# A two-layer gated attention network on one core: the hand-over from the first stage to the expert stage, with fifteen loads moved from GpSimd's DMA queue to SyncE's, one load moved later and one wait added on GpSimd

## The chip, the cores and the metric

One core of a Trainium2 chip runs the whole program. The metric is the device time of one execution in microseconds (us); smaller is better. The core has TensorE (PE in the rows; PEld is its weight load), VectorE (DVE), ScalarE (ACT), GpSimd (POOL) and SyncE (SP, which here only issues DMAs). Sixteen DMA engines carry the transfers of all queues. Queue q1 holds what SP issues, q10 what ACT issues, q0 what POOL issues.

## The reference, cut to what matters

The input is x, 4 x 512 rows of 256 float32 numbers, and a context of the same shape. Four residual blocks follow one another:

```python
x = x + tanh(g_xattn[0]) * L0_xattn(layernorm(x), ctx, ...)      # attention over the 16 places of a head, per row
x = x + tanh(g_ffn[0])   * L0_ffn(layernorm(x), ...)             # shared expert + one of 8 experts per row (argmax)
x = x + tanh(g_xattn[1]) * L1_xattn(ctx, ctx, layernorm(x), ...) # attention over the 512 rows of a batch entry
x = x + tanh(g_ffn[1])   * L1_ffn(layernorm(x), ...)             # butterfly weights, 256 -> 1024 -> 256
```

An expert is `gelu(x @ w1) * (x @ w2) @ w3` with 256 x 1024, 256 x 1024 and 1024 x 256 weights (3 MB). Each row goes through the shared expert and through the expert with the largest of 8 logits. The butterfly block multiplies small 2 x 2 weights stage by stage; the kernel folds these stages into dense matrices once, from tables of coefficients.

## The kernel before, in words

Rows are cut into 16 tiles of 128 (`T = 16`). The order of the work is written out by hand for each engine; engines meet at semaphores alone.

**First stage (about 0 to 331 us of the profiled span).** `sweep_a` runs a software pipeline over the tiles. For one tile: the first attention (VectorE multiplies into `PRODQ`, 128 x 4096, and sums it, `score_sums`; GpSimd multiplies into `PRODV`, two halves `hf` of 128 x 2048, and adds halves of each), then the second layer norm (`normal_rows` on VectorE writes the normal rows `XH`), then the shared expert (`up_half`, `down_rows` on TensorE). The reciprocal square root of the norm is a one-column operation on GpSimd (`second_root`). SyncE writes each `XH` to the DRAM tensor `normal_rows` (`keep_rows(n)`). Tiles are numbered 0 to 15; semaphore `xn2_ready` reaches n + 1 when the normal rows of tile n stand in `XH`. The last tiles, 13 to 15, are finished by `drain` on each engine: on TensorE the attention output of a tile (`attended`, which waits for `a_ready`), `out_rows`, `up_half`, `normal_rows` (two transposes of `XH`), `gate`, `down_rows`; on VectorE also the choice of experts and the sorting of rows by expert (`choices`, `places`, `one_hots`, `inverse`), which ends in `INV`, the list of rows for the expert tiles.

**Expert stage (to about 620 us).** The sorted rows make up to 23 tiles (`NT = 23`). GpSimd's `fetch(n)` gathers the 128 rows of expert tile n from `normal_rows` by an indirect DMA into `XS[n % 2]`; TensorE transposes them (semaphore `sT_done`), ScalarE copies the transposes (`XST`, `sT_sb`), TensorE multiplies them by `SLOT`, of which there are three (`SLOTS`): experts 0 and 1 stand in slots 0 and 1 long before, and slot 2 holds the shared expert, so expert 2 can be loaded only when TensorE has finished the last `down_rows` (`y_done` at 16). In the step for tile t, TensorE's order is: transposes of the product of tile t - 2, transposes of the gathered rows of tile t, the products of tile t - 1, the down product of tile t - 2.

**Work on the side in the expert stage.** Fourteen tables for the butterfly weights (`load_coef`, 2 x 7 DMAs into `COEF`, which is the memory of `PRODQ`) and the contraction weights `Z` (1 MB, in the memory of `PRODV`) come in at the hand-over. GpSimd multiplies the tables out between the gathers (`grow_up` after `fetch(1)`, then `fetch(2)`, `grow_down`, `fetch(3)`, `fetch(4)`, and so on); VectorE does one quarter of a stage on `Z` in each of the first four expert steps (`first_stage`).

The last stages, second attention and folded butterfly block, take the rest.

Of the kernel before, what the change touches and what calls it, by code (L numbers as in the profile page):

```python
# [27 lines left out]
P = 128  # L28
B, L, D = 4, 512, 256
T = B * L // P  # L30
# [10 lines left out]
LOW, HIGH = 7, 3  # L41
# [3 lines left out]
def spread(v, axis, n):  # L45

    shape = list(v.shape)
    shape[axis] = n
    return v.broadcast_to(shape)


def build(nc, x, ctxT, gates, wq0, wkv0, wo0, wg, wexp, wk1, wv1, wq1, wo1, bv1, bq1, bo1,
          weT, be, uplow, uphigh, upb, dnlow, dnhigh, wc, bc, db, out):
    with ExitStack() as ctx:
# [105 lines left out]
        COEF = [flatA[:, r * 2048:(r + 1) * 2048] for r in range(2)]  # L160
        WEFF = flatA[:, 0:KD * F].rearrange("p (k f) -> p k f", k=KD)
        MDN = flatA[:, KD * F:2 * KD * F].rearrange("p (c d) -> p c d", c=KF)
        Z = flatV[:, 0:KF * D].rearrange("p (c d) -> p c d", c=KF)
# [19 lines left out]
        at = [0]  # L183
# [56 lines left out]
        z_in = sem("z_in")  # L240
# [60 lines left out]
        LAG = 4  # L301
# [83 lines left out]
        @block.sync  # L385
        def _(sp):
            def load_tile(j, par):
                t = 2 * j + par
                if not (isinstance(j, int) and j == 0):

                    sp.wait_ge(tile_in[par], 32 * j)
                    sp.wait_ge(s["kv_done"], t - 1)
                sp.dma_start(X[:, t, :], x[bass.ds(t * P, P), :]).then_inc(tile_in[par], 16)
                sp.dma_start(CTX[:, par, :, :],
                             ctxT[:, bass.ds(t * P, P)].rearrange("(k p) t -> p k t", p=P))\
                    .then_inc(tile_in[par], 16)

            load_tile(0, 0)
            for w, src in ((WQ0, wq0), (WKV0, wkv0)):
                sp.dma_start(w[:, :, :], src.rearrange("(k p) n -> p k n", p=P)).then_inc(w_in, 16)  # L400
            load_tile(0, 1)
            for w, src in ((WO0, wo0), (WG, wg)):
                sp.dma_start(w[:, :, :], src.rearrange("(k p) n -> p k n", p=P)).then_inc(wg_in, 16)
            sp.dma_start(GATE[:, :], gates.partition_broadcast(P)).then_inc(wg_in, 16)
            sp.dma_start(SLOT[:, 2, :], wexp[NE]).then_inc(slot_in[2], 16)

            def keep_rows(n):

                sp.wait_ge(s["xn2_ready"], n + 1)
                sp.dma_start(xs[n * P:(n + 1) * P, :], XH[:, n % 2, :]).then_inc(xh_out[n % 2], 16)  # L410

            for t in range(2, T):
                if t >= LAG + 1:
                    keep_rows(t - LAG - 1)
                load_tile(t // 2, t % 2)
            for w, src in ((WK1, wk1), (WV1, wv1), (WQ1, wq1), (WO1, wo1)):
                sp.dma_start(w[:, :, :], src.rearrange("(k p) n -> p k n", p=P)).then_inc(c_in, 16)
            for n, src in enumerate((bo1, bc, db)):
                sp.dma_start(BIAS[:, 1 + n, :], src.partition_broadcast(P)).then_inc(c_in, 16)
            with nc.allow_non_contiguous_dma("biases and coefficients by partition"):  # L420
                sp.dma_start(BQ[:, :], bq1.rearrange("(k p) -> p k", p=P)).then_inc(c_in, 16)
                sp.dma_start(BV[:, :], bv1.rearrange("(k p) -> p k", p=P)).then_inc(c_in, 16)
                sp.dma_start(UPB[:, :], upb.rearrange("(k p) -> p k", p=P)).then_inc(c_in, 16)
                for n, src in enumerate((uphigh, dnhigh)):
                    sp.dma_start(HIC[:, n, :, :, :], src.rearrange(
                        "s (q p) c -> p s q c", p=P)).then_inc(c_in, 16)
                sp.dma_start(WET[:, :, 0:D], weT.rearrange("(c p) d -> p c d", p=P)).then_inc(c_in, 16)
                sp.dma_start(WET[:, :, D:W1P], be.rearrange("(c p o) -> p c o", p=P, o=1))\
                    .then_inc(c_in, 16)
            sp.dma_start(SLOT[:, 0, :], wexp[0]).then_inc(slot_in[0], 16)  # L430
            sp.dma_start(SLOT[:, 1, :], wexp[1]).then_inc(slot_in[1], 16)


            for n in range(T - LAG - 1, T):
                keep_rows(n)
            sp.wait_ge(s["y_done"], T)
            sp.dma_start(SLOT[:, 2, :], wexp[2]).then_inc(slot_in[2], 16)
            sp.wait_ge(tables, 1)
            for n in range(SLOTS, NE):

                base = sp.value_load(BASEI[0:1, n - 2:n - 1], min_val=1, max_val=NT + 1)
                sp.wait_ge(slot_uses, base)
                sp.dma_start(SLOT[:, n % SLOTS, :], wexp[n]).then_inc(slot_in[n % SLOTS], 16)

            sp.wait_ge(rt_ps, KF)

            def load_ctx(b):
                if b >= 2:
                    sp.wait_ge(c["sc_done"], TB * (b - 1))
                sp.dma_start(CTXB[b % 2], ctxT[:, b * L:(b + 1) * L].rearrange("(k p) t -> p k t", p=P))\  # L450
                    .then_inc(ctx_in[b % 2], 16)

            def outputs(b):
                for q in range(TB):
                    tile = b * TB + q
                    sp.wait_ge(c["fin_ready"], tile + 1)
                    sp.dma_start(out[tile * P:(tile + 1) * P, :], X[:, tile, :]).then_inc(stored, 16)

            load_ctx(0)
            load_ctx(1)  # L460
            for b in range(2, B):
                load_ctx(b)
                outputs(b - 2)
            outputs(B - 2)
            outputs(B - 1)
            sp.wait_ge(stored, 16 * T)
# [3 lines left out]
        def _(gp):  # L470
# [20 lines left out]
            def second_root(n):  # L491

                gp.wait_ge(s["ln2_eps"], n + 1)
                gp.tensor_tensor(MV[:, 1, 3:4], MV[:, 1, 2:3], MHALF[:, :], ALU.pow).then_inc(s["ln2_rstd"], 1)

            def step(of):
                if (t3 := of(3)) is not None:
                    second_root(num(t3))
                if (t0 := of(0)) is not None:
                    gp.wait_ge(s["ln1_eps"], num(t0) + 1)  # L500
                    gp.tensor_tensor(MV[:, 0, 3:4], MV[:, 0, 2:3], MHALF[:, :], ALU.pow)\
                        .then_inc(s["ln1_rstd"], 1)
                if (t1 := of(1)) is not None:
                    n, par = num(t1), t1[1]
                    gp.wait_ge(s["exp_done"], n + 1)
                    gp.wait_ge(s["kv_sb"], n + 1)
                    for hf in range(2):
                        if not first(t1, 1):

                            gp.wait_ge(s["av_read"], 2 * (n - 1) + hf + 1)  # L510
                        H2 = NH // 2
                        o = PRODV[:, :].rearrange("p (f i h j) -> p f i h j", f=2, i=DK, h=H2)[:, hf]
                        pr = spread(PR[:, par, :].rearrange("p (i o j) -> p i o j", i=DK, o=1), 2, H2)
                        v = KV[:, par, D + hf * H2 * DK:D + (hf + 1) * H2 * DK]
                        v = spread(v.rearrange("p (o h j) -> p o h j", o=1, j=DK), 1, DK)
                        gp.tensor_tensor(o, pr, v, ALU.mult).then_inc(s["av_prod"], 1)  # L516
                        gp.wait_ge(s["av_prod"], 2 * n + hf + 1)
                        gp.tensor_tensor(o[:, :, :, 0:DK // 2], o[:, :, :, 0:DK // 2], o[:, :, :, DK // 2:DK],  # L518
                                         ALU.add).then_inc(s["av_half"], 1)
                        if hf == 0 and isinstance(n, int) and n == T - 1:  # L520
                            second_root(T - 2)

            sweep_a(gp, step)
            second_root(T - 1)

            def load_coef(n, src):

                for k in range(LOW):
                    w = 16 << k
                    at = 16 * ((1 << k) - 1)  # L530
                    if n == 0:
                        v = src[k].rearrange("(b r w) -> b r w", b=P >> k, r=1)
                        v = spread(v, 1, 1 << k)
                    else:
                        w = 1024 >> k
                        at = 16 * ((64 >> k) - 1)
                        v = src[k].rearrange("(b r w) -> b r w", b=1, r=2 << k)
                        v = spread(v, 0, 64 >> k)
                    gp.dma_start(COEF[n][:, at:at + w], v).then_inc(coef_in[n], 16)


            gp.wait_ge(s["a_ready"], T)
            load_coef(0, uplow)
            load_coef(1, dnlow)
            gp.dma_start(Z, wc.rearrange("(c p) d -> p c d", p=P)).then_inc(z_in, 16)

            def fetch(n):

# [1313 lines left out]
```

## Time and profile before

| | us |
|---|---|
| median of 3 runs | 862.6 |
| lowest, highest | 861.34, 864.33 |
| the profiled execution's own time | 863.65 |
| its span | 861.7 |
| TensorE busy | 750.8 (87%) |
| VectorE busy | 483.4 (56%) |
| GpSimd busy | 386.4 (45%) |
| ScalarE busy | 254.1 (29%) |

The span is the time from the first to the last instruction that the profiler recorded; the execution's time is a little longer. Busy time of an engine other than the one that sets the end costs nothing by itself. The matmul records are pipelined: a group's busy time and the distance between two starts differ by some tenths of a us.

### The profile page before, as it was taken

The numbers are of one execution on the slowest core, as the hardware profiler recorded it, in microseconds if no ns is written. First come the engines' busy times: TensorE is split into PE (matmuls) and PEld (weight loads), VectorE is DVE, ScalarE is ACT, GpSimd is POOL, SyncE is SP. The second block draws the span as 40 slices with busy tenths as digits, with TensorE's granted clock in tenths as the row PEclk, the third lists the DMA queues.
The fourth block names the chain that finished last, engine by engine and source line by source line (L and its number), as shares of the span: only waits on it lengthen the run. The fifth ranks groups of instructions, "written<-read, shape, count | busy, mean of one in ns | idle before, by whom it ended". The sixth has DMA issues, their size and how long they took to land.

```text
span 861.7 us, 11168 instructions
## 1 busy us (share of the span) xinstructions
PE 750.8 (87%) x3843; PEld 571.6 (66%) x3843; DVE 483.4 (56%) x837; ACT 254.1 (29%) x458; POOL 386.4 (45%) x318
## 2 busy tenths in 40 slices
PE   4259999999998795998999999999957888899977
PEld 1138878878887694565666666666645677797856
DVE  4889999999999653321111111111456767566442
ACT  1013333333333110222222212221333361636432
POOL 1688988998998646060333333340062323000000
PEclk9569999999999897999999999999979999899979
DMA  7000001001290046013044423000011001000000
GB/s 244 12 19 19 19 20 38 18 18 37 82 347 12 13 101 217 19 59 124 19 172 172 171 97 148 19 25 8 19 49 39 12 21 53 1 20 6 14 13 25
DMA packets 30633, 54.24 MB, mean 63 GB/s; under 512 B 9972, under 2 KB 26148, under 8 KB 29440
## 3 DMA queue, kind: packets, MB, share of 16 engines
q1 hardware_dynamic: 23168, 42.41, 14.0%
q0 software_dynamic: 4112, 8.26, 3.9%
q10 hardware_dynamic: 3312, 3.02, 1.0%
q8 instruction: 27, 0.44, 0.2%
q14 instruction: 14, 0.11, 0.0%
HBM read 46.45 MB, written 7.21 MB: 62 GB/s over the span
## 4 chain that ended last, share of the span: by engine, by line
PE 46%; DVE 9%; issue 7%; DMA 3%; ACT 3%; POOL 1%; POOLq 0%; ACTq 0%; DVEq 0%
PE bank L687 31%; PE bank L951 11%; PE bank L694 3%; DMA expert_rows<-YS 2%; DVE SLOT L1698 2%; DVE PRODV_r L1627 1%; DMA SLOT<-wexp 1%; DVE STC L1684 1%; ACT XST L1194 1%; DVE SLOT_r L1627 1%; DVE XH L1355 1%; ACT SLOT_r L1209 0%; POOL SLOT L659 0%; PE bank L938 0%; ACT XS L1194 0%
## 5 line engine op out<-in xcount | busy, mean ns | idle before, releaser
L687 PE MATMUL bank<-SLOT,XST 128*128 x368 | 163.0, 596 | 0.0
L516 POOL TENSOR_TENSOR PRODV<-SHARED 128x2048 f32<-128x2048 f32 x32 | 144.6, 4517 | 27.9 <-DVE bank L1367 27.9
L687 PE MATMUL bank<-SLOT,HA 128*128 (+1 forms) x624 | 145.9, 388 | 3.3 <-DVE HA L1489 2.0
L687 PEld LDWEIGHTS bank<-SLOT,HA 128*128 128x128 f32 x624 | 120.0, 194 | 38.2 <-issue 12.4
L687 PEld LDWEIGHTS bank<-X2T,SLOT 128*128 128x128 f32 x1024 | 120.7, 194 | 1.6
L687 PE MATMUL bank<-X2T,SLOT 128*128 128x128 f32 x1024 | 121.0, 277 | 0.0
L687 PEld LDWEIGHTS bank<-SLOT,XST 128*128 128x128 f32 x368 | 68.6, 192 | 77.8 <-issue 77.8
L1596 DVE TENSOR_TENSOR SHARED<-bank,G 128x512 f32<-128x512 f32 x46 | 31.8, 692 | 135.9 <-PE bank L687 135.9
L551 POOL DMA_INDIRECT XS<-normal_rows,INV x23 | 23.5, 1022 | 140.0 <-PE bank L694 124.4
L665 POOL TENSOR_TENSOR RS<-VE,MHALF 128x4 f32<-128x4 f32 x8 | 10.4, 1297 | 152.0 <-DVE VE L1690 152.0
L1289 DVE TENSOR_TENSOR PRODQ<-bank,SHARED 128x4096 f32<-128x4096 f32 x16 | 70.7, 4416 | 13.2 <-PE bank L687 13.2
L518 POOL TENSOR_TENSOR PRODV<-PRODV 128x1024 f32<-128x1024 f32 x32 | 74.7, 2333 | 2.5
L1298 DVE TENSOR_REDUCE bank<-PRODQ 128x256 f32<-128x4096 f32 x16 | 70.7, 4419 | 0.1
L1587 DVE COPY HA<-bank 128x512 f32<-128x512 f32 x23 | 15.9, 691 | 72.8 <-PE bank L694 72.8
L1168 ACT ACTIVATE G<-bank 128x512 f32<-128x512 f32 x46 | 27.5, 597 | 91.9 <-PE bank L687 91.8
L951 PE MATMUL bank<-SLOT_r,PRODQ_r 128*128 128x512 f32 x128 | 43.4, 422 | 5.5 <-ACT XS L1194 4.0
L951 PE MATMUL bank<-PRODQ_r,SLOT_r 128*128 128x256 f32 x128 | 36.9, 288 | 5.3 <-DVE PRODV_r L1627 5.3
L687 PE MATMUL bank<-WKV,SHARED 128*128 128x512 f32 x64 | 34.8, 672 | 7.2 <-DMA WKV<-wkv 7.2
L1174 ACT ACTIVATE YS<-bank 128x256 f32<-128x256 f32 x23 | 8.8, 383 | 107.1 <-PE bank L687 91.0
L1083 ACT ACTIVATE G<-bank 128x512 f32<-128x512 f32 x32 | 19.1, 597 | 68.8 <-PE bank L687 68.7
L659 POOL DMA_INDIRECT SLOT<-expert_rows,POS x16 | 15.6, 974 | 50.6 <-DMA expert_rows<-YS 46.3
L1367 DVE TENSOR_REDUCE bank<-PRODV 128x128 f32<-128x1024 f32 x32 | 36.7, 1191 | 0.4 <-POOL PRODV L518 0.4
(237 smaller groups left out, 1307.8 us busy)
## 6 DMA issues: line engine op xcount, KB each, us to landing
SLOT<-wexp SPq DMA_DIRECT2D x9, 3072.0 KB, 11.9
expert_rows<-YS ACTq DMA_DIRECT2D x23, 128.0 KB
X<-x SPq DMA_DIRECT2D x16, 128.0 KB, 2.2
SHARED<-ctxT SPq DMA_DIRECT2D x16, 128.0 KB, 2.3
normal_rows<-XH SPq DMA_DIRECT2D x16, 128.0 KB, 1.7
WET<-ctxT SPq DMA_DIRECT2D x4, 512.0 KB, 8.7
out<-X SPq DMA_DIRECT2D x16, 128.0 KB
WET<-weT SPq DMA_DIRECT2D x1, 1024.0 KB, 5.9
```

The lines of the kernel that those rows point to most:

```text
L516: gp.tensor_tensor(o, pr, v, ALU.mult).then_inc(s["av_prod"], 1)
L518: gp.tensor_tensor(o[:, :, :, 0:DK // 2], o[:, :, :, 0:DK // 2], o[:, :, :, DK // 2:DK], ALU.add).then_inc(s["av_half"], 1)
L551: gp.indirect_dma_start(out=XS[:, n % 2, :], out_offset=None, in_=xs, in_offset=bass.IndirectOffsetOnAxis(ap=INV[:, n:n + 1], axis=0))\
L687: last = pe.matmul(dst, lhs(k), rhs(k), start=(k == 0), stop=(k == chunks - 1))
L694: last = pe.transpose(bank[:, k * P:(k + 1) * P], src[:, k * P:(k + 1) * P], IDENT[:, :])
L951: last = pe.matmul(dst, f32r(a), f32r(b), start=(k == 0 and n == 0), stop=(k == chunks - 1 and n == 2))
L1083: act.activation(G[:, hf * 512:(hf + 1) * 512], PB[6][:, :], ACT.Gelu).then_inc(s["gelu_done"], 1)
L1168: act.activation(G[:, hf * 512:(hf + 1) * 512], PB[1 + hf][:, :], ACT.Gelu)\
L1289: dve.tensor_tensor(PRODQ[:, :].rearrange("p (i j h) -> p i j h", i=DK, j=DK), spread(PB[1][:, 0:D].rearrange("p (i o h) -> p i o h", i=DK ...
L1298: dve.tensor_reduce(SCP.rearrange("p (i j) -> p i j", i=DK), PRODQ[:, :].rearrange("p (i j h) -> p i j h", i=DK, j=DK), AX.X, ALU.add)\
L1367: dve.tensor_reduce(aov[:, :, hf * H2:(hf + 1) * H2], PRODV[:, :].rearrange("p (f i h j) -> p f i h j", f=2, i=DK, h=H2) [:, hf, :, :, 0:D ...
L1596: dve.tensor_tensor(HB[:, t1[1], hf * 512:(hf + 1) * 512], PB[3 + hf][:, :], G[:, hf * 512:(hf + 1) * 512], ALU.mult).then_inc(e["b_mult"], 1)
```

## The change

Three things are changed, all at the hand-over.

1. The fourteen table loads and the load of `Z` are issued by SyncE instead of GpSimd. The tables wait for `scores` at 16 (the last `score_sums`, after which `PRODQ` is free) instead of `a_ready` at 16; `Z` still waits for `a_ready` at 16 (the last read of `PRODV`). In SyncE's order they stand between `keep_rows(13)` and `keep_rows(14)`.
2. The load of expert 2 into slot 2 waits for `sT_done` at 2 (the transposes of expert tiles 0 and 1) as well as for `y_done` at 16.
3. GpSimd waits, between the two halves of the last attention product of tile 15, for `xn2_ready` at 15: the normal rows of tile 14.

```diff
@@ block.sync @@
+            def load_coef(n, src):
...
+                    sp.dma_start(COEF[n][:, at:at + w], v).then_inc(coef_in[n], 16)
+
-            for n in range(T - LAG - 1, T):
+            for n in range(T - LAG - 1, T - 2):
+                keep_rows(n)
+            sp.wait_ge(s["scores"], T)
+            load_coef(0, uplow)
+            load_coef(1, dnlow)
+            sp.wait_ge(s["a_ready"], T)
+            sp.dma_start(Z, wc.rearrange("(c p) d -> p c d", p=P)).then_inc(z_in, 16)
+            for n in range(T - 2, T):
                 keep_rows(n)
             sp.wait_ge(s["y_done"], T)
+            sp.wait_ge(e["sT_done"], 2)
             sp.dma_start(SLOT[:, 2, :], wexp[2]).then_inc(slot_in[2], 16)
@@ block.gpsimd @@
                         if hf == 0 and isinstance(n, int) and n == T - 1:
                             second_root(T - 2)
+                            gp.wait_ge(s["xn2_ready"], T - 1)
 
             sweep_a(gp, step)
             second_root(T - 1)
-
-            def load_coef(n, src):
...
-            gp.wait_ge(s["a_ready"], T)
-            load_coef(0, uplow)
-            load_coef(1, dnlow)
-            gp.dma_start(Z, wc.rearrange("(c p) d -> p c d", p=P)).then_inc(z_in, 16)
```

How the instructions stand on two engines. SyncE's DMA queue before, from the load of expert 1 (`SLOT<-wexp`) and the writes of tiles 11 to 15 (`normal_rows<-XH`) on:

```order
L431 DMA SLOT<-wexp 128x6144
L410 DMA normal_rows<-XH 128x256 [waits xn2_ready] x5
L437 DMA SLOT<-wexp 128x6144 [waits y_done]
L441 TENSOR_LOAD BASEI [waits tables]
L441 ISA x2
```

SyncE's queue after, in the two places where something is put in; the first piece is the beginning of the tables, the second the end of them, `Z` (`PRODV<-wc`), the writes of tiles 14 and 15, and the load of expert 2:

```order
L410 DMA normal_rows<-XH 128x256 [waits xn2_ready] x3
L447 DMA PRODQ<-uplow 128x16 [waits scores]
L447 DMA PRODQ<-uplow 128x1x32
...
L447 DMA PRODQ<-dnlow 128x1x32
L447 DMA PRODQ<-dnlow 128x16
L455 DMA PRODV<-wc 128x8x256 [waits a_ready]
L410 DMA normal_rows<-XH 128x256 [waits xn2_ready] x2
L460 DMA SLOT<-wexp 128x6144 [waits sT_done,y_done]
```

Fifteen DMA issues now stand between the writes of tiles 13 and 14, and the load of expert 2 has a second wait.

GpSimd before, from the root for tile 14 (L494) over the last half product of tile 15 (L516, L518) and the root for tile 15 to the tables, of which the first and last stand here, and the first two gathers (L551):

```order
L494 TENSOR_TENSOR MV<-MV,MHALF 128x1 [waits ln2_eps]
L516 TENSOR_TENSOR PRODV<-SHARED 128x2048 [waits av_read]
L518 TENSOR_TENSOR PRODV<-PRODV 128x128x8 [waits av_prod]
L494 TENSOR_TENSOR MV<-MV,MHALF 128x1 [waits ln2_eps]
L539 DMA PRODQ<-uplow 128x16 [waits a_ready]
...
L539 DMA PRODQ<-dnlow 128x16
L545 DMA PRODV<-wc 128x8x256
L551 DMA XS<-normal_rows,INV 128x256 [waits xh_out1,xh_out0,inv_ok]
L551 DMA XS<-normal_rows,INV 128x256
```

GpSimd after, the same place:

```order
L517 TENSOR_TENSOR MV<-MV,MHALF 128x1 [waits ln2_eps]
L539 TENSOR_TENSOR PRODV<-SHARED 128x2048 [waits av_read,xn2_ready]
L541 TENSOR_TENSOR PRODV<-PRODV 128x128x8 [waits av_prod]
L517 TENSOR_TENSOR MV<-MV,MHALF 128x1 [waits ln2_eps]
L554 DMA XS<-normal_rows,INV 128x256 [waits xh_out1,xh_out0,inv_ok]
L554 DMA XS<-normal_rows,INV 128x256
```

The last half product has the added wait, and nothing stands any more between the last root and the first gather. TensorE, VectorE and ScalarE keep their instructions and their order.

## Rows read from the trace of the kernel before

**Rows 1.** Busy us by stretch: PE, PEld, DVE, ACT, POOL; PE clock, DMA share, GB/s

```profile
331.00:341.00 10.00, 1.56 (x7) 0.74 (x6) 2.38 (x7) 0.38 (x1) 7.42 (x10) 0.79 0.88 341
```

**Rows 2.** Chain that ended last, in order of time: start us, us, what

```profile
288.78 4.58 DVE XH L1355
...
310.63 4.17 PE bank L687 x20
...
331.46 9.08 DMA SLOT<-wexp
```

**Rows 3.** VectorE's timeline: start us, us, line, operation, tiles [idle before]

```profile
278.79 0.41 DVE L1355 TENSOR_SCALAR XH<-X,MV 128x256 f32<-128x256 f32 x1 [0.61 <-POOL MV L494]
...
296.90 0.42 DVE L1375 TENSOR_TENSOR AO<-bank,RI 128x256 f32<-128x256 f32 x1
```

**Rows 4.** GpSimd's timeline around 289 us

```profile
288.71 4.49 POOL L516 TENSOR_TENSOR PRODV<-SHARED 128x2048 f32<-128x2048 f32 x1
```

**Rows 5.** TensorE's timeline around 290 us

```profile
293.41 0.69 PE L694 MATMUL bank<-IDENT,XH 128*128 128x128 f32 x2 [3.11 <-DVE XH L1355]
```

**Rows 6.** TensorE's timeline, tiles 14 and 15 of the first stage

```profile
304.38 0.38 PE L694 MATMUL bank<-IDENT,AO 128*128 128x128 f32 x2
...
306.20 3.73 PE L687 MATMUL bank<-X2T,SLOT 128*128 128x128 f32 x32
309.77 0.38 PE L694 MATMUL bank<-IDENT,XH 128*128 128x128 f32 x2
```

**Rows 7.** GpSimd's timeline: the load of Z and the first three gathers

```profile
317.15 1.18 POOL L545 DMA_DIRECT2D PRODV<-wc  x1
327.66 1.08 POOL L551 DMA_INDIRECT XS<-normal_rows,INV  x1 [9.34 <-DVE INV L1550]
329.04 0.99 POOL L551 DMA_INDIRECT XS<-normal_rows,INV  x1 [0.30 <-issue]
...
338.39 0.98 POOL L551 DMA_INDIRECT XS<-normal_rows,INV  x1 [2.01 <-PE bank L694]
```

**Rows 8.** TensorE's timeline, the first expert tiles

```profile
337.43 0.69 PE L694 MATMUL bank<-IDENT,XS 128*128 128x128 f32 x2 [6.00 <-DMA XS<-normal_rows,INV]
340.55 0.69 PE L694 MATMUL bank<-IDENT,XS 128*128 128x128 f32 x2 [2.44 <-DMA SLOT<-wexp]
341.03 8.28 PE L687 MATMUL bank<-SLOT,XST 128*128 x16
...
350.66 0.38 PE L694 MATMUL bank<-IDENT,XS 128*128 128x128 f32 x2
350.88 7.03 PE L687 MATMUL bank<-SLOT,XST 128*128 x16
```

**Rows 9.** DMA issues by line, KB each, median us from issue to landing

```profile
SLOT<-wexp SPq DMA_DIRECT2D x9, 3072.0 KB, 11.9
...
normal_rows<-XH SPq DMA_DIRECT2D x16, 128.0 KB, 1.7
...
PRODV<-wc POOLq DMA_DIRECT2D x1, 1024.0 KB, 19.0
```

**Rows 10.** One line's instructions: gathers, all 23

```profile
DMA to landing us min/median/max: 2.8/3.6/11.5
```

**Rows 11.** The load of an expert issued at 431.5, and its landing

```profile
L443 SPq DMA_DIRECT2D SLOT<-wexp x1: 327/327/327, 431.5 to 431.5; - x1
...
DMA to landing us min/median/max: 10.7/10.7/10.7
```

**Rows 12.** The gather issued at 432.8, and its landing

```profile
L551 POOL DMA_INDIRECT XS<-normal_rows,INV x1: 1015/1015/1015, 432.8 to 432.8; - x1
...
DMA to landing us min/median/max: 8.2/8.2/8.2
```

**Rows 13.** SyncE's timeline: the dearest of its issues

```profile
237.02 1.52 SPq L425 DMA_DIRECT2D HIC<-dnhigh  x1
```

**Rows 14.** Two us after the first hole (columns as in rows 1)

```profile
292.00:294.00 2.00, 0.59 (x2) 0.29 (x2) 2.00 (x3) 0.00 (x0) 1.92 (x2) 0.58 0.00 0
```

More of the change, by code:

```diff
@@ L431, in _ @@
             sp.dma_start(SLOT[:, 1, :], wexp[1]).then_inc(slot_in[1], 16)
-            for n in range(T - LAG - 1, T):
+            def load_coef(n, src):
+                for k in range(LOW):
+                    w = 16 << k
+                    at = 16 * ((1 << k) - 1)
+                    if n == 0:
+                        v = src[k].rearrange("(b r w) -> b r w", b=P >> k, r=1)
+                        v = spread(v, 1, 1 << k)
+                    else:
+                        w = 1024 >> k
+                        at = 16 * ((64 >> k) - 1)
+                        v = src[k].rearrange("(b r w) -> b r w", b=1, r=2 << k)
+                        v = spread(v, 0, 64 >> k)
+                    sp.dma_start(COEF[n][:, at:at + w], v).then_inc(coef_in[n], 16)
[7 more added lines that the diff above has]
+            for n in range(T - 2, T):
                 keep_rows(n)
             sp.wait_ge(s["y_done"], T)
+            sp.wait_ge(e["sT_done"], 2)
             sp.dma_start(SLOT[:, 2, :], wexp[2]).then_inc(slot_in[2], 16)
@@ L521, in step @@
                             second_root(T - 2)
+                            gp.wait_ge(s["xn2_ready"], T - 1)
             sweep_a(gp, step)
             second_root(T - 1)
-            def load_coef(n, src):
[L528 to L539, printed above, removed]
-            gp.wait_ge(s["a_ready"], T)
-            load_coef(0, uplow)
-            load_coef(1, dnlow)
-            gp.dma_start(Z, wc.rearrange("(c p) d -> p c d", p=P)).then_inc(z_in, 16)
             def fetch(n):
```

## The prediction, made before the changed kernel was run

> **What bounds the kernel now.** TensorE is the busiest engine, so I read first which stretches leave it idle. The table of busy time by stretch has one hole at the hand-over: from 331 to 341 us TensorE works 1.56 of 10 us while the DMA engines are busy 0.88 of the time [rows 1]. Then the chain of waits, which shows what the end depends on there. It has two pieces that are not TensorE's: VectorE's `XH` operation at 288.78, 4.58 us long, and at 331.46 a wait of 9.08 us put down to a DMA [rows 2]. These are the two places that the change touches.
>
> First place. The same VectorE operation took 0.41 us one tile earlier [rows 3], and GpSimd's half product of 4.49 us had started at 288.71, 0.07 us before it [rows 4]. 288.71 + 4.49 = 293.20, and VectorE's operation ends at 293.36. So VectorE stood still until GpSimd was done. TensorE had nothing for 3.11 us until 293.41 [rows 5], that is since 290.30.
>
> Second place. Gathers 0 and 1 are issued at 327.66 and 329.04 [rows 7], and their transposes start at 337.43 and 340.55 [rows 8]: 9.8 and 11.5 us, where the fastest gather lands 2.8 us after its issue and the middle one 3.6 [rows 10]. Ahead of them on GpSimd's queue is `Z`, issued at 317.15, which lands 19.0 us later, at 336.2 [rows 7, 9]; and the load of expert 2 starts at 331.46, when TensorE's last `down_rows` ends. I read the wait of TensorE from 331.46 as these two transfers together.
>
> **The change, part by part.** The sums are made in the profiled execution, 863.65 us.
>
> *The wait on GpSimd.* GpSimd is done with the root of tile 14 before 288.71. It now starts the half product when `XH` stands, 288.78 + 0.41 = 289.19, plus about 0.05, so 0.53 us late. `XH` is done 4.17 us earlier, but TensorE is free only at 290.30, so the start of the transposes gains 3.11. More follows. After the idle time the granted clock was 0.58 of full speed from 292 to 294 [rows 14], near the lower level of 1.2 GHz, and from 293.41 to the transposes of tile 15's attention at 304.38 [rows 6] TensorE took 10.97 us. The same work for the next tile: transposes at 309.77 [rows 6] to the end of gate and down product at 310.63 + 4.17 = 314.80 [rows 2] is 5.03, and an `up_half` is 309.77 - 306.20 = 3.57 [rows 6]; together 8.60. Without the idle time I expect that figure, 2.37 less. Gain so far 3.11 + 2.37 = 5.5.
>
> What the wait makes late: the product of tile 15, the reduction and `AO`. `AO` ends at 296.90 + 0.42 = 297.32 [rows 3]; with 0.53 that is 297.9. TensorE will want it at 304.38 - 5.5 = 298.9. It is hidden by 1.0 us, and costs its excess over that if GpSimd starts later than I take it. The root of tile 15 and all of the sorting come 5.5 earlier, since they follow TensorE.
>
> *The tables and Z on SyncE.* SyncE gets 15 issues. One of its issues with broken-up rows cost 1.52 us, the dearest of those shown [rows 13]; fifteen of them are at most 23 us, and from `keep_rows(13)` at about 279.3 the fourteen tables are out by 300.6 at the latest. `Z` waits for `AO` (297.9) and goes at 298 to 301. Behind it stand the writes of tiles 14 and 15. Tile 15's rows stand when TensorE takes them, 309.77 - 5.5 = 304.3 at the latest [rows 6]; a write takes 1.7 us [rows 9], so it lands at 306, or behind a `Z` that takes 19.0 us as before [rows 9], at about 320. The first gather is issued at 327.66 - 5.5 = 322.2. So even that bound is hidden. What else is queued behind the tables on SyncE is the load of expert 2, later still.
>
> On GpSimd the 15 issues vanish; it was idle from their end to 327.66, so by themselves they are worth nothing. What is worth something is the empty queue: gathers 0 and 1 are issued at 322.2 and 323.5 and should land after 2.8 to 3.6 us, a little over the least, 3.2. The last `down_rows` ends at 331.46 - 5.5 = 326.0; gather 0 is there. Gather 1 lands at 326.8, and its transposes start then instead of at 340.55. The products of tile 0 start 0.22 later at full clock (350.66 to 350.88 [rows 8]), at 327.0 instead of 341.03. They took 8.28 us where the next tile's took 7.03 [rows 8], after the hole in which the mean clock was 0.79 [rows 1]; with at most 0.8 us of idle time ahead of them now I take the full speed, 1.25 less. Up to here the gain is 14.0 + 1.25 = 15.3.
>
> *The load of expert 2 behind the gathers.* It is issued when tile 1's transposes are done, about 327.1, and an expert's load took 10.7 us with little beside it [rows 11] and 11.9 in the median of nine [rows 9], so it lands at 337.8 to 339.0. Its own user, expert 2's first tile, is several expert tiles away, each longer than the 9.6 us from 341.03 to 350.66, so it is hidden. But gather 2 is not: GpSimd issued gather 2 when `grow_up` was over, at 338.39 - 2.01 = 336.4, 7.3 us after gather 1 [rows 7]; with the tables long there it is 6.7, so at 330.2, three us into the load. The nearest rows say what happens then. A gather issued at 432.8, 1.3 us after a load, landed after 8.2, at 441.0, while the load landed at 431.5 + 10.7 = 442.2 [rows 11, 12]: the gather comes out with the end of the load. So gather 2 lands at 336.6 to 339.0; I take 337.6. TensorE wants it at 327.0 + (350.66 - 341.03) - 1.25 = 335.4 and must take it before the products of tile 1. A new stall of 2.2 us (1.2 to 3.6). Before, gather 2 had room until 350.66.
>
> The Trainium skill, page "DMA: Bandwidth & Descriptors", section "Queues, rings and completion order", speaks against this: each DMA engine takes turns between the queues that have work, packet by packet. By that rule a small gather would pass a large load and gather 2 would land in time, which is the rival "gather 2 slips through" below. The row of 8.2 us is against it, and I go by the row.
>
> *Clock after the new stall.* After 3.11 us of idle time the clock fell [rows 5, 14] and the loss was 2.37; a stall of 2.2 may or may not do it. Bounds 0 and 2.4, taken 1.2. `grow_up` now lies beside the first `first_stage` on VectorE; either may hold the other up for a us or two, but TensorE needs neither before about 331.
>
> **Sum.** 5.5 + 8.5 (gathers) + 1.25 (clock at tile 0) - 2.2 - 1.2 = 11.9 us, so 851.8 for the profiled execution. That execution was 1.05 above the median of the runs shown, so I give 850.7. What comes later follows TensorE's own progress (each later load waits for a slot, each gather for a transposition), so I let the gain stand to the end.
>
> **The rivals** (times against the median, 862.6).
> - *Gather 2 slips through.* It lands after 3.6 us as most do, or the load's queue lets it by. For it speaks the page above, and that gather 2 is issued 3 us, not 1.3, after the load; against it the 8.2 us. No new stall, no clock loss: 15.3, 847.3.
> - *The wait on GpSimd gives nothing*: `AO` is late by what `XH` gains, or another wait ends there. For it: the spare of 1.0 us is thin. Only the gathers' part is left: 6.4, 856.2.
> - *The gathers are as late as before*: they are slow by themselves as the first of their kind, or the tables' data still fill the engines. For it: before, gathers 0 and 1 took 9.8 and 11.5 us. Against: the middle one of all 23 takes 3.6 [rows 10]. Only 5.5 is left: 857.1.
> - *Slower than before.* The writes of tiles 14 and 15 are stuck behind tables and `Z` on SyncE, and all gathers wait for them. It costs from a landing at 322.2 on, and eats the whole gain of 11.9 when tile 15's rows land after 334; for a loss of 0.3% (2.6 us) after 336.7, over 30 us after their issue. At 340 the time would be 866. For it only that `Z` alone took 19.0 us on GpSimd's queue.
> - *No effect* needs two of these together.
>
> **How the numbers follow.** A difference of 0.3%, 2.6 us, is about what a measurement of this kernel tells from none. Chances: the forecast 0.52 (848.0 to 853.4 by its bounds: stall 1.2 to 3.6, clock 0 to 2.4, gather 1 half a us either way), gather 2 slips through 0.20, the wait on GpSimd gives nothing 0.11, the gathers are late 0.11, slower 0.03, no effect 0.03. The range reaches from below the first rival to just below the last two that are faster: 846.5 to 857.0. Faster 0.94, same 0.03, slower 0.03.
>
> **What would show it.** `XH` of tile 14 about 0.4 us and TensorE with no hole at 290; the transposes of tile 15's attention near 298.9; the first gathers 3 us from issue to landing; the products of tile 0 near 327 at 7.0 us; then a hole of 1 to 4 us before the transposes of tile 2, ended by gather 2 or the load of expert 2. The prediction is wrong if `AO` or tile 15's rows set the pace, if gather 2 lands before 335.4, or if a stall between 341 and 620 grows by what was gained.

## The result, and the profile after

Four runs of the changed kernel have a median of 851.5 us (850.98 to 852.32), against 861.97 for four of the kernel before taken with them: ratio 0.986 with a 95% interval of [0.981, 0.991], so faster, by 10.5 us. The forecast was 850.7, that is 11.9 less than 862.6, range 846.5 to 857.0. The profiled execution took 852.0, its span is 850.2; the forecast for it was 851.8. Busy times: TensorE 747.5 us (88%), VectorE 483.2, GpSimd 377.4, ScalarE 254.4.

First place. VectorE's timeline after the change (start us, us, line, operation, tiles, idle before), what answers to [rows 2, 3]; the last rows are `first_stage(0)`:

```profile
288.35 0.41 DVE L1358 TENSOR_SCALAR XH<-X,MV 128x256 f32<-128x256 f32 x1 [0.34 <-POOL MV L517]
...
297.03 0.42 DVE L1378 TENSOR_TENSOR AO<-bank,RI 128x256 f32<-128x256 f32 x1
...
323.94 2.13 DVE L1636 TENSOR_SCALAR WORK<-PRODV,HIC 128x256 f32<-128x256 f32 x4
326.11 1.44 DVE L1638 TENSOR_TENSOR PRODV<-WORK 128x256 f32<-128x256 f32 x1
327.47 2.56 DVE L1639 TENSOR_TENSOR PRODV<-WORK 128x256 f32<-128x256 f32 x1
```

GpSimd's timeline, for [rows 4, 7]:

```profile
288.84 4.49 POOL L539 TENSOR_TENSOR PRODV<-SHARED 128x2048 f32<-128x2048 f32 x1 [0.53 <-DVE XH L1358]
...
321.43 1.23 POOL L554 DMA_INDIRECT XS<-normal_rows,INV  x1 [19.30 <-DVE INV L1553]
322.97 0.95 POOL L554 DMA_INDIRECT XS<-normal_rows,INV  x1 [0.30 <-issue]
...
330.54 0.99 POOL L554 DMA_INDIRECT XS<-normal_rows,INV  x1 [0.79 <-POOL PRODV L582]
```

TensorE's timeline, for [rows 5, 6, 8]:

```profile
289.69 0.38 PE L697 MATMUL bank<-IDENT,XH 128*128 128x128 f32 x2
...
298.12 0.38 PE L697 MATMUL bank<-IDENT,AO 128*128 128x128 f32 x2
...
319.81 3.70 PE L690 MATMUL bank<-SLOT,HA 128*128 128x256 f32 x16
325.51 0.43 PE L697 MATMUL bank<-IDENT,XS 128*128 128x128 f32 x2 [2.00 <-issue]
328.29 0.66 PE L697 MATMUL bank<-IDENT,XS 128*128 128x128 f32 x2 [2.34 <-issue]
328.74 9.22 PE L690 MATMUL bank<-SLOT,XST 128*128 x16
...
339.79 0.44 PE L697 MATMUL bank<-IDENT,XS 128*128 128x128 f32 x2 [0.32 <-DMA XS<-normal_rows,INV]
340.11 7.13 PE L690 MATMUL bank<-SLOT,XST 128*128 x16
```

The hole before the transposes of `XH` is gone. Those of the gathered rows come 9 to 12 us earlier, but each has a gap of 2.0 and 2.34 us ahead of it in which TensorE waited for nothing that the profile shows ("issue"). What its queue did there is in the rows of the line that reads a tile's slot numbers from the table `TAB` into registers (`placed(n)`, four per tile; ns min/median/max, then the first and last start):

```profile
L841 PEldq TENSOR_LOAD <-TAB x92: 294/300/488, 322.7 to 578.4; - x92
L841 PEldq FUSED_REGOPS  x92: 146/146/165, 323.3 to 578.9; - x92
L841 PEldq SEQ_ASSERT  x92: 18/18/32, 323.5 to 579.1; - x92
```

Four times 300 + 146 + 18 ns is 1.86 us: `placed(0)` stands ahead of tile 0's transposes, `placed(1)` between them and tile 1's. Before, the same loads ran while TensorE waited for the gathers.

What `placed(0)` itself waits for is not TensorE's last product but the semaphore `tables`, which VectorE raises behind the last step of the sorting (`BASEI`). In the changed kernel this is 0.83 us before the last `down_rows` ends:

```profile
322.52 0.16 DVE L1571 TENSOR_SCALAR BASEI<-BASE 1x8 int32<-1x8 f32 x1
```

The register loads start at 322.7, and the transposes of tile 0 2.83 us behind the end of `BASEI`.

Two stretches of the table of busy time (PE, PEld, DVE, ACT, POOL; clock, DMA share, GB/s) show the clock before and behind the gaps; 0.50 is the lower of its two levels, 1.2 of 2.4 GHz:

```profile
320.00:324.00 4.00, 3.51 (x16) 2.74 (x15) 2.75 (x15) 0.00 (x0) 2.24 (x3) 1.00 0.13 37
...
326.00:328.00 2.00, 0.00 (x0) 0.00 (x0) 1.97 (x3) 0.36 (x1) 1.92 (x2) 0.57 0.00 0
328.00:330.00 2.00, 1.71 (x4) 1.13 (x5) 2.00 (x1) 0.38 (x1) 1.75 (x1) 0.50 0.12 25
330.00:332.00 2.00, 2.00 (x3) 0.67 (x2) 0.03 (x1) 0.00 (x0) 1.37 (x3) 0.50 1.11 307
```

Gather 2, issued at 330.54, has this row in the view of its line:

```profile
DMA to landing us min/median/max: 9.2/9.2/9.2
```

SyncE's queue, for [rows 13] and the `Z` of [rows 7]:

```profile
279.10 4.35 SPq L447 DMA_DIRECT2D PRODQ<-uplow  x7
283.50 16.83 SPq L447 DMA_DIRECT2D PRODQ<-dnlow  x7
300.37 0.43 SPq L455 DMA_DIRECT2D PRODV<-wc  x1
300.85 2.17 SPq L410 DMA_DIRECT2D normal_rows<-XH  x2
329.02 0.33 SPq L460 DMA_DIRECT2D SLOT<-wexp  x1
```

**A ruler for all runs.** Before 286 us the kernels are the same, yet starts differ by 1 to 2 us from one profiled execution to the next. So I measure inside each trace from T0, the start of VectorE's `XH` operation of tile 14, to P1, the start of tile 1's products. From P1 on nothing differs much: the span ends 510.8 us after P1 before and 510.1 after; over all runs below it is 508.6 to 512.0.

| from T0, us | before | after | earlier by | forecast |
|---|---|---|---|---|
| transposes of tile 15's attention | 15.60 | 9.77 | 5.8 | 5.5 |
| end of the last `down_rows` | 42.66 | 35.16 | 7.5 | 5.5 |
| start of tile 0's products | 52.25 | 40.39 | 11.9 | 14.0 |
| end of tile 0's products | 60.53 | 49.61 | 10.9 | 15.3 |
| P1 | 62.10 | 51.76 | 10.3 | 13.1 |

The forecast for P1 is 15.3 less the stall of 2.2; its last term, 1.2 for the clock, was to be paid in the products of tile 1 and later, behind P1. The total came out near the forecast, the path to it did not: 2.0 ahead of it at the last `down_rows`, then 4.1 lost until the products of tile 0 start and 2.2 more in them, then 1.6 won back before P1, which is 2.8 late. Behind P1 the 1.2 us were not lost.

### The profile page after: what moved, and what is told of

It reads as the page before. It is cut to its first block, busy times and chain, and to the rows that moved or that the text cites. A ratio compares the mean times of both kernels' runs of the same rounds, so it can differ in the third digit from the quotient of the medians.

```text
span 850.2 us, 11170 instructions
## 1 busy us (share of the span) xinstructions
PE 747.5 (88%) x3843; PEld 569.4 (67%) x3843; DVE 483.2 (57%) x837; ACT 254.4 (30%) x458; POOL 377.4 (44%) x303
## 4 chain that ended last, share of the span: by engine, by line
PE 44%; issue 9%; DVE 8%; DMA 3%; ACT 3%; POOL 2%; POOLq 0%; ACTq 0%; DVEq 0%
PE bank L690 30%; PE bank L954 11%; PE bank L697 3%; DMA expert_rows<-YS 2%; DVE SLOT L1701 2%; DVE PRODV_r L1630 1%; DMA XS<-normal_rows,INV 1%; POOL PRODV L582 1%; DVE STC L1687 1%; ACT XST L1197 1%; DVE SLOT_r L1630 1%; DMA normal_rows<-XH 1%; ACT SLOT_r L1212 0%; POOL SLOT L662 0%; PE bank L941 0%
## 5 line engine op out<-in xcount | busy, mean ns | idle before, releaser
L690 PE MATMUL bank<-SLOT,HA 128*128 (+1 forms) x624 | 142.4, 381 | 3.3 <-DVE HA L1492 2.0
L690 PEld LDWEIGHTS bank<-SLOT,HA 128*128 128x128 f32 x624 | 117.4, 190 | 37.2 <-issue 12.4
L668 POOL TENSOR_TENSOR RS<-VE,MHALF 128x4 f32<-128x4 f32 x8 | 10.4, 1297 | 151.8 <-DVE VE L1693 151.8
L1171 ACT ACTIVATE G<-bank 128x512 f32<-128x512 f32 x46 | 27.5, 597 | 93.1 <-PE bank L690 93.1
## 6 DMA issues: line engine op xcount, KB each, us to landing
WET<-ctxT SPq DMA_DIRECT2D x4, 512.0 KB, 8.6
```

Of the source, the lines that this page charges most:

```text
L690: last = pe.matmul(dst, lhs(k), rhs(k), start=(k == 0), stop=(k == chunks - 1))
L1171: act.activation(G[:, hf * 512:(hf + 1) * 512], PB[1 + hf][:, :], ACT.Gelu)\
```

## The experiments

The times are medians of 5 to 10 runs (four for the kernels before and changed). The ratio is against runs of the kernel before on the same chip; their medians lie between 860.37 and 861.97. P1 - T0 is from the one profiled execution, and this lies far from the median in the run without GpSimd's wait (3.0 us below it) and in the one with TensorE kept busy (4.1 above).

| kernel | us | ratio [95%] | P1 - T0 | tile 0's products |
|---|---|---|---|---|
| before | 861.97 | | 62.10 | 8.28 |
| changed | 851.5 | 0.986 [0.981, 0.991] | 51.76 | 9.22 |
| GpSimd's wait alone | 863.52 | 1.003 [1.001, 1.005] | 64.48 | 9.33 |
| load behind gathers alone | 860.43 | 0.999 [0.996, 1.002] | 62.24 | 8.60 |
| changed, without GpSimd's wait | 858.86 | 0.996 [0.992, 0.999] | 55.91 | 7.13 |
| changed, load not held | 853.85 | 0.990 [0.987, 0.994] | 53.56 | 9.56 |
| wait and load, tables on GpSimd | 855.17 | 0.993 [0.991, 0.996] | 54.53 | 8.46 |
| changed, registers later | 848.65 | 0.985 [0.982, 0.989] | 49.84 | 8.30 |
| changed, gather 2 earlier | 850.17 | 0.987 [0.983, 0.991] | 51.21 | 9.25 |
| both of these | 847.52 | 0.983 [0.979, 0.987] | 48.58 | 8.37 |
| registers and load later | 848.19 | 0.984 [0.981, 0.988] | 48.66 | 8.46 |
| *on one chip:* changed | 851.75 | 0.990 [0.987, 0.993] | 51.67 | 8.89 |
| both, again | 848.75 | 0.987 [0.984, 0.990] | 50.15 | 9.94 |
| both, and TensorE busy | 845.9 | 0.982 [0.978, 0.986] | 49.32 | 7.13 |

### The parts of the change

**GpSimd's wait alone, on the kernel before.**

```diff
                             second_root(T - 2)
+                            gp.wait_ge(s["xn2_ready"], T - 1)
```

> The kernel before with only the wait on GpSimd added; tables, Z and the load of expert 2 stay as they were. My theory: half of the gain of the whole change comes from this wait alone, because it frees VectorE's normal rows of tile 14 (0.41 us in place of 4.57), closes TensorE's hole of 3.1 us at 290 and keeps its clock up. Expected: about 5.8 us less than before, 856 to 857, the transposes of tile 15's attention near 298.5 in place of 304.38, the late gathers at the hand-over unchanged. Rival (the wait gives back what it gains, since the last half product starts later): within 1 us of before.

`XH` took 0.41 us and the attention of tile 15 came 5.8 us earlier, as in the changed kernel. The end did not come earlier, where I had expected 5.8 us less: 863.52 against 861.5 for the kernel before on that chip, and P1 is 2.4 us later. TensorE's timeline of this kernel has the hole again, longer:

```profile
338.49 0.69 PE L695 MATMUL bank<-IDENT,XS 128*128 128x128 f32 x2 [15.31 <-DMA XS<-normal_rows,INV]
341.15 0.66 PE L695 MATMUL bank<-IDENT,XS 128*128 128x128 f32 x2 [1.97 <-issue]
```

With the last `down_rows` over at 323.2, the load of expert 2 goes out at 323.22, while the tables and `Z` are still coming in on GpSimd's queue: `Z`, issued at 310.59, lands after 27.5 us where it took 19.0 [rows 9], and gather 0 stands behind it:

```profile
DMA to landing us min/median/max: 27.5/27.5/27.5
```

**The load behind the gathers alone, on the kernel before.**

```diff
             sp.wait_ge(s["y_done"], T)
+            sp.wait_ge(e["sT_done"], 2)
```

> The kernel before with only the load of expert 2 put behind the first two gathers; tables and Z stay on GpSimd. My theory: the queue of tables and Z keeps gather 0 late at 337.4 (Z lands at 336.2), perhaps a little sooner with the load out of the way, gather 1 follows within 1.5 us, and gather 2, issued at 338.4, is caught by the load: 0 to 2 us less than before, 860 to 862. Rival (the load of expert 2 is what made the gathers late, tables and Z are not): gathers 0 and 1 land after about 3 us each and the time falls by 6 us or more.

No difference in time, and P1 in the same place (62.24 against 62.10). The transposes of tile 0 still start 9.8 us after the issue of gather 0, with no load beside it: in the kernel before, what holds it is the backlog of its own queue. The DMA engines themselves were nearly idle while it waited, as the table of busy time of this run shows:

```profile
332.00:338.00 6.00, 0.31 (x2) 0.29 (x2) 0.81 (x3) 0.00 (x0) 5.33 (x6) 0.65 0.10 34
```

My reading of the wait from 331.46 "as these two transfers together" was wrong for that kernel.

**The changed kernel without GpSimd's wait, and with the load not held back.**

```diff
-                            gp.wait_ge(s["xn2_ready"], T - 1)
```

> The changed kernel without the wait on GpSimd: tables and Z on SyncE, load of expert 2 behind the gathers. My theory: what is left is the hand-over's part, 5 to 6 us less than before, 856 to 857; the first two gathers land after 2.8 to 3.0 us. Rival (the parts need each other, for instance because the clock is low after the first hole): under 3 us less than before.

VectorE's `XH` is 4.58 us again and P1 comes 4.15 us later than in the changed kernel; 858.86 against 851.5. Against the kernel before on its chip the median is 2.6 us less (3.6 by the ratio), and not the 5 to 6 that I expected: it is nearer the rival's "under 3". The profile doesn't show why: its execution took 855.82, 3.0 less than the median, and in it P1 comes 6.2 us earlier than before. So within the change the wait is worth 4.15 us by that execution and 7.4 by the medians; my forecast had 5.5.

```diff
             sp.wait_ge(s["y_done"], T)
-            sp.wait_ge(e["sT_done"], 2)
```

> The changed kernel with the load of expert 2 waiting for y_done alone, as before. My theory (a gather issued near a load comes out with the load's end): the load goes at about 323.4, gather 1, issued at 323.0, lands with it at about 334 in place of 325.8, the products of tile 1 start at about 344 in place of 340.1, and the time is 3 to 4 us above the changed kernel, about 855. Rival (the queues take turns and small gathers pass): gather 1 lands by 327 and the time is that of the changed kernel or 1 us less, since gather 2 is also nearer the load's end.

P1 comes 1.8 us later, and the median is 2.4 higher. The load goes out at 321.67, 0.57 us behind gather 1 (321.10), and TensorE's timeline has:

```profile
323.66 0.64 PE L696 MATMUL bank<-IDENT,XS 128*128 128x128 f32 x2 [2.02 <-issue]
328.42 0.69 PE L696 MATMUL bank<-IDENT,XS 128*128 128x128 f32 x2 [4.12 <-DMA XS<-normal_rows,INV]
```

Gather 1 landed after 7.3 us and not, as gathers issued behind a load do, near the load's end at 332.1. Neither theory nor rival had this (11 us, or under 4). In return gather 2, issued 7.0 us behind the load, was back in 3.7 us, just as the load ended, and there was no stall at tile 2.

**Wait and load together, the tables still on GpSimd.** The two edits above on the kernel before.

> The kernel before with the wait on GpSimd and the load of expert 2 behind the first two gathers; tables and Z stay on GpSimd. It asks why the wait alone (e1) gained nothing. My theory now: in e1 the last down product ended 8 us earlier, so the 3 MB load of expert 2 started at 323.2 amid the backlog of Z (issued at 310.6, landed at 338.1, 27.5 us) and held Z and gather 0 up. With the load behind the gathers Z takes about 19 us again and lands near 330, gather 0 near 331, and the transposes of tile 2 minus the VectorE operation at 288 come to 55 to 57 us, 5 to 7 less than before: about 856. Rival (the backlog on GpSimd's queue alone does it): Z still takes over 25 us, and the time is that of e1, about 863.

This settles the first run: the wait alone lost 2.4 us, with the load held back as well the two gain 7.6. `Z` is back at 18.3 us; gather 0 is still slow, 8.2 us, behind it:

```profile
328.23 0.69 PE L696 MATMUL bank<-IDENT,XS 128*128 128x128 f32 x2 [6.12 <-DMA XS<-normal_rows,INV]
```

The tables on SyncE take that hole away and bring the last 2.8 us (54.53 to 51.76). So the parts don't add: from P1 - T0, the wait is worth -2.4 alone and 4.15 within the change; the load's place nothing alone, 9.95 on top of the wait (64.48 to 54.53), 1.8 within the change.

### What the forecast had missed

**The register loads of tile n + 1 are issued a step later**, when the step of tile n + 1 has transposed its rows, so that they stand ahead of its products and not ahead of its transposes.

```diff
-                if t0 is not None and num(t0) + 1 < NT:
-                    held_for[num(t0) + 1] = placed(num(t0) + 1)
+                if t0 is not None and num(t0) >= 1:
+                    held_for[num(t0)] = placed(num(t0))
```

> The changed kernel with one edit on TensorE: the four register loads for expert tile n + 1, which stood at the end of step n, now stand at the end of step n + 1, behind the products of tile n. Only between the transposes of gathers 0 and 1 does that matter, where TensorE had 2.34 us without work although gather 1 had landed. My theory (the four loads of 300 + 146 + 18 ns each are that gap, and the low clock at tile 0 follows from the two gaps): transposes of tile 1 near 326.4 in place of 328.29, products of tile 0 near 326.6; but gather 2 still comes out with the load of expert 2, near 337.5, so the products of tile 1 start near 338 in place of 340.11: 2 us less than the changed kernel, about 849.5. Rival (the gap is something else, the landing of the gather or of ScalarE's copy): no difference, 851.5.

```profile
325.55 0.43 PE L697 MATMUL bank<-IDENT,XS 128*128 128x128 f32 x2 [2.01 <-issue]
326.55 0.66 PE L697 MATMUL bank<-IDENT,XS 128*128 128x128 f32 x2 [0.56 <-ACT XST L1163]
327.00 8.30 PE L690 MATMUL bank<-SLOT,XST 128*128 x16
337.85 0.44 PE L697 MATMUL bank<-IDENT,XS 128*128 128x128 f32 x2 [1.03 <-DMA XS<-normal_rows,INV]
```

The gap of 2.34 us before tile 1's transposes became 0.56, waiting for ScalarE's copy. The products start at the forecast 327.0, and the stall at gather 2 grows from 0.32 to 1.03 us, since TensorE is there sooner. P1 comes 1.9 us earlier; 848.65.

**Gather 2 ahead of `grow_up`**, so that it is issued before the load of expert 2.

```diff
             fetch(1)
+            fetch(2)
...
-            fetch(2)
```

> The changed kernel with gather 2 issued before grow_up instead of behind it, so that it is on its way before the load of expert 2. My theory: gather 2 waits for the transposes of tile 0, is issued at about 326 and lands by 329.5, ahead of the load; it was on the path by 0.3 us only, so the time is 0.3 us less, 851.2, not to be told from the changed kernel. Rival (gather 2 is the bound of the hand-over, as my forecast had it with a stall of 2.2 us): 2 us less, 849.5.

Gather 2, issued at 325.62, landed after 3.4 us instead of 9.2:

```profile
DMA to landing us min/median/max: 3.4/3.4/3.4
```

The stall is gone, and it had been 0.32: P1 is 0.55 us earlier, and 850.17 against 851.5 can't be told apart.

**Both.**

> Both edits: register loads of tile 1 behind the products of tile 0, and gather 2 before grow_up. My theory: with the register loads out of the way and gather 2 early, the transposes of tile 2 start 8.4 to 10 us after the products of tile 0 at 326.6, at 335 to 337, in place of 339.79: 3 to 4.9 us less than the changed kernel, 846.6 to 848.5, more than the sum of the two edits alone (2.3). Rival (something else ends there, for instance the clock stays low after the hole before gather 0): under 2.5 us less.

847.52; P1 3.2 us earlier than in the changed kernel. Gather 2 is now worth 1.3 us of it (49.84 to 48.58), since there is a stall to remove: from the end of tile 0's products to P1 it is 2.9 us with later registers alone and 1.6 with both edits.

**Later registers, gather 2 where it was, and the load held back until tile 2's rows are transposed.**

```diff
-            sp.wait_ge(e["sT_done"], 2)
+            sp.wait_ge(e["sT_done"], 3)
```

> Register loads of tile 1 behind the products of tile 0, gather 2 where the change has it, but the load of expert 2 one gather later (sT_done at 3). My theory: gather 2, issued at 330.5 with nothing beside it, lands at about 333.5; the time is that of the kernel with both edits within 0.5 us, 846.6 to 848.5. Rival (gather 2 is slow by itself beside grow_up, not through the load): it lands after 9 us as in the changed kernel and nothing is gained over the first edit, 849.5.

P1 - T0 48.66, as with both. Here gather 2 is issued where it always was, beside `grow_up`, and lands after 3.5 us. Gathers 3 and 4, issued at 337.30 and 338.60 beside the load of 337.49, take 9.0 and 10.0. So the slowness belongs to the load, not to gather 2 or to what GpSimd does.

**On one chip: the changed kernel, both edits, and both edits with TensorE kept busy** while it waits for the gathers.

```diff
             drain()
+            for n in range(5):
+                pe.matmul(PB[0][:, :], IDENT[:, :], WKV0[:, n % 2, :], start=True, stop=True)
```

The five products are read by nothing; the profile has two records for each.

> The changed kernel once more, on the chip of the two kernels with both edits, for a direct comparison: 851 to 852.

> The kernel with both edits once more, beside the changed kernel: 3 to 4 us less than it, about 848.

> The kernel with both edits (register loads of tile 1 later, gather 2 early) and five matmuls of 128x512 more on TensorE, whose result nothing reads, between the last down product and the register loads of tile 0: they fill the hole of 2 us. It measures the clock term. My theory: the products of tile 0 took 8.3 us there in place of 7.0 since the clock fell in that hole; with the hole filled they take 7.0 to 7.2 and the time falls by about 1.2 us against the kernel with both edits (profile: transposes of tile 2 minus the VectorE operation at 288 is 47.3 in place of 48.6). Rival (the clock falls all the same, or the five matmuls are in the way of the transposes): no gain, or up to 1 us slower.

Both edits are 3.0 us under the changed kernel (848.75, 851.75), and they were 4.0 under it before (847.52, 851.5), though the intervals of the two ratios overlap a little here. With the matmuls TensorE's timeline and the table of busy time read:

```profile
323.49 4.46 PE L838 MATMUL bank<-WKV,IDENT 128*128 128x512 f32 x10
327.78 0.38 PE L697 MATMUL bank<-IDENT,XS 128*128 128x128 f32 x2
328.72 0.41 PE L697 MATMUL bank<-IDENT,XS 128*128 128x128 f32 x2 [0.56 <-ACT XST L1165]
329.11 7.13 PE L690 MATMUL bank<-SLOT,XST 128*128 x16
```

```profile
326.00:328.00 2.00, 2.00 (x7) 0.85 (x5) 0.01 (x1) 0.00 (x0) 0.00 (x0) 1.00 0.00 0
328.00:330.00 2.00, 1.44 (x6) 0.69 (x5) 0.00 (x0) 0.77 (x2) 1.47 (x3) 1.00 0.00 0
```

The clock stays at 1.00 and tile 0's products take 7.13 us. But the matmuls took 4.46 us where I had planned some 2, and pushed the transposes back: P1 - T0 is 49.32, between the 48.58 and 50.15 of the two runs of both edits. (Those two, the same kernel, differ in tile 0's products by 1.6 us, by how long the clock was low.) In this execution, what the clock gave back went to the matmuls. It took 849.95; the median of 845.9 is lowest of all, with three executions at 841.6 to 843.5 and three at 848.3 to 850.0. The profile is of the upper group, so what the lower group did stays open. The ratio of 0.982 is hardly below the 0.983 of the first run of both edits, and its interval overlaps those of both runs: no shown gain. The best kernel that I can vouch for is that with both edits, 3 to 4 us under the changed one.

## Why the prediction came out, step by step

**Right.**
- *The wait on GpSimd.* `XH` 0.41 us, no hole at 290, GpSimd 0.53 us late as worked out (the bracket of its row), `AO` ended at 297.45 and was hidden. At tile 15's attention 5.8 us were gained, forecast 5.5.
- *The Trainium skill*, page "SBUF — State Buffer", section "SBUF: two separate sides", says that VectorE and GpSimd share a port pair by an exclusive lock, held for a whole instruction. The 4.57 against 0.41 us agree, and so does `first_stage(0)`, which now lies beside `grow_up`: 6.1 us where it took about 2.0 before. That was hidden, as foreseen: VectorE's next operation waits for TensorE until 334.66.
- *SyncE.* Fourteen table issues took 21 us and were out by 300.3; the bound was 300.6. That it held was luck: it took 1.52 us as the dearest issue, and one took 8.6 and another 3.3, while most took under 0.9. `Z` landed 6.1 us after its issue, the rows of tile 15 by 307.1, 14 us before the first gather was issued.
- *The gathers behind an empty queue* landed after 3.0 and 2.8 us; forecast 2.8 to 3.6.
- *Gather 2* (issued 330.54, forecast 330.2) came in with the load: 9.2 us later, at 339.7, the load at 340.7. Without a load beside it, it took 3.4 and 3.5. By the rule of the Trainium skill ("DMA: Bandwidth & Descriptors", section "Queues, rings and completion order") that each DMA engine takes turns between its queues packet by packet, a small gather would pass, as the prediction read it; these runs disagree with that.

**Wrong, and hidden in a sum that was right.**
- *"Gather 1 lands at 326.8, and its transposes start then."* The step left out what TensorE's own queue does between the two pairs of transposes. Gather 1 had landed at 325.8, the transposes started at 328.29, behind the four register loads. The run with later registers shows it: it moved them 1.76 us earlier, by T0. This is the step that failed.
- *"The last `down_rows` ends at 326.0; gather 0 is there."* It ended 2.0 us before that by T0, but the transposes of tile 0 came where the forecast had them (37.16 us behind T0, forecast 37.2): they waited for `placed(0)`, and this for VectorE's `BASEI`. In all nine traces with the tables on SyncE and no added matmuls they start 2.83 to 2.85 us behind the end of `BASEI`, whenever TensorE is done. The kernel without GpSimd's wait shows it best, as its last `down_rows` is 1.7 us longer: the gap of TensorE shrinks to 0.34 and the 2.85 stay.

```profile
325.39 0.16 DVE L1570 TENSOR_SCALAR BASEI<-BASE 1x8 int32<-1x8 f32 x1
328.40 0.43 PE L696 MATMUL bank<-IDENT,XS 128*128 128x128 f32 x2 [0.34 <-issue]
```

- *"With at most 0.8 us of idle time ahead of them now I take the full speed, 1.25 less."* There were 2.0 and 2.34 us of idle time, the clock was at 0.50 in the first four us of tile 0's products, and they took 9.22, not 7.03. The run with TensorE kept busy shows that the idle time is what it hung on (7.13). In these traces it goes with the first gap and not with the second alone: without GpSimd's wait, with gaps of 0.34 and 2.32, they took 7.13 too. By themselves these 2.2 us were hardly on the path, since gather 2 came 0.3 us behind them.
- *A new stall of 2.2 us, and 1.2 for the clock after it.* Both follow from a TensorE that is there at 335.4. It was there at 339.47, so the stall was 0.32 and the clock did not fall. The cost had been paid ahead of it. With the registers out of the way the stall is 1.03. Moving `placed(0)`, or raising `tables` sooner, was not tried.
- *The gain at the last `down_rows`* was 7.5 us, not 5.5: it took 3.70 us where it had taken 5.39 (below).

In sum, from the ledger, against the forecast of 13.1 at P1: 2.0 more at the last `down_rows`, which `placed(0)` took back whole; 2.1 more lost until the products of tile 0 start, most of it by `placed(1)`; 2.2 lost in them; 1.6 won by the smaller stall. 13.1 + 2.0 - 4.1 - 2.2 + 1.6 is 10.4, the 10.3 of the table. The same 2.8 us can be read along the other path: the load of expert 2 went out 2.35 us later by T0 than forecast, since it waits for the transposes of tile 1, and gather 2 came with it. Behind P1 the forecast took off 1.2 for the clock; measured are 0.7 us gained there and 0.4 from an earlier T0, no more than the spread between executions. So the total of the profiled execution, 852.0 against 851.8, is right by luck: an error of 2.8 at P1 met 1.2 that were not lost and 1.1 of spread.

Two slips in the prediction's own figures: the slow end of its bounds, with a stall of 3.6, clock 2.4 and gather 1 half a us late, is 853.8 and not 853.4; and its range, 846.5 to 857.0, holds the times of two rivals (847.3 and 856.2), so that the time alone could not have told the mechanism from them.

**The rivals.** "Gather 2 slips through" fell with the 9.2 us, "the gathers are late as before" with the 3.0, "the wait gives nothing" with the 4.15 us (7.4 by the medians) of the kernel without it. But the 11 in 100 for that one were given for a wrong reason: alone the wait gives nothing, by a collision of the load with the queue of tables that I had not on the list. I had treated the parts as a sum.

## What to carry to other kernels

When a wait goes, list everything on the waiting engine's own queue between its neighbours, register loads too, and what each of them waits for: under a long wait they cost nothing, and afterwards they are the path. Price parts of a change together where one decides when another's transfer starts: here a part alone was worth -2.4 us and with its fellows 4. Put small gathers that are wanted soon ahead of a large load, not beside it, and don't count on a sum that is right to have right terms.

## What the runs showed of the hardware that I had not expected

**A gather beside a 3 MB load comes in with the load's end.** Issued 1.1 to 3.3 us behind a load they took 10.0 (gather 4 with the load held longest), 9.2 and 9.1 (gather 2 in the two runs of the changed kernel), 8.4 (without GpSimd's wait), 8.2 [rows 12] and 7.2 us (with the registers later). Issued ahead of one the delay fades: 9.0 us when 0.2 us ahead, 7.3 at 0.57, 6.1 at 0.78 (TensorE kept busy), 4.4 and 4.3 at 1.0 (both edits), 3.4 at 2.8. With no load beside them, 2.7 to 3.5. What in the DMA engines does this, no run here shows.

**The clock fell under a busy TensorE.** In the kernel before, 36 us after the first hole began and after 26 us at a clock of 1.00, the table of busy time has:

```profile
324.00:326.00 2.00, 1.94 (x16) 1.83 (x16) 2.00 (x4) 0.00 (x0) 0.00 (x0) 1.00 1.01 229
326.00:328.00 2.00, 2.00 (x8) 1.62 (x8) 1.72 (x10) 0.00 (x0) 0.34 (x1) 0.62 0.33 86
328.00:330.00 2.00, 2.00 (x7) 1.62 (x6) 1.00 (x5) 0.00 (x0) 1.70 (x2) 0.53 0.34 96
```

The last `down_rows` took 5.39 us there, and also in the two other kernels in which VectorE's `XH` is held up (load alone, change without the wait). In all eleven traces with the wait it took 3.70 at full clock. TensorE has the same instructions ahead of it in both. That the lower clock goes with the hole at `XH` is seen in all fourteen traces; why it does stays open.

**Issuing can be slow.** The first seven table issues took SyncE 0.43 to 0.70 us each, the other seven 0.53 to 8.6, the last the longest (ns min/median/max):

```profile
L447 SPq DMA_DIRECT2D PRODQ<-dnlow x7: 528/1120/8633, 283.5 to 291.7; - x7
```

The write of tile 14's rows, which stood at 288.76, waited behind it until 300.85, and `Z` until 300.37; nobody wanted either before 321, so it cost nothing.
